# Operand loads split between cross attention's contexts, and the latent stage's transposes moved one slot behind their scores

## The reference, cut to what matters

```
x = layernorm(x + L0_xattn(x, ctx, ctx))       # 16 heads of 16, 361 context rows per batch
...
# L1_xattn: latents = x (100 rows per batch), ctx has 361 rows, 16 heads of 64
xn, ln = layer_norm(ctx), layer_norm(latents)
q = ln @ Wq;  k, v = split(concat(xn, ln) @ Wkv)          # 461 keys
sim = where(mask, (q * scale) @ k^T, -max)
out = layer_norm((softmax(sim) @ v) @ Wout)
x = layernorm(x + out)
```

## Time and profile before

| | |
|---|---|
| median of 3 runs | 2555.2 us |
| the profiled execution | 2563.16 us |
| its span in the trace | 2561.5 us |
| TensorE busy | 2135.1 us (83%) |
| VectorE, ScalarE, GpSimd busy | 1355.6, 1128.6, 474.4 us |
| granted clock, mean | 0.912 of full speed |
| cross attention, about | 590 to 1035 us |
| latent attention, about | 1359 to 2289 us |

### The profile page before, as it was taken

One profiled execution on the slowest core, in us unless ns is written; L12 is line 12 of the kernel. 1 busy time (PEld: TensorE's weight loads), 2 busy tenths in 40 slices (PEclk: granted clock), 3 DMA queues, 4 the chain that ended last, 5 costly groups with the idle time before them and its releaser, 6 DMA issues. The chain is left out here.

```text
span 2561.5 us, 48525 instructions
## 1 busy us (share of the span) xinstructions
PE 2135.1 (83%) x17362; PEld 1314.8 (51%) x17363; DVE 1355.6 (53%) x3264; ACT 1128.6 (44%) x2404; POOL 474.4 (19%) x533
## 2 busy tenths in 40 slices
PE   1888888864999999777777999999999999963992
PEld 0454555442666665554443555655555555552661
DVE  1577777751455555358883455555555555432223
ACT  0566666650555555135552444444444444420110
POOL 2455555510000000224440000000000000003002
PEclk9789999975999999779997999999999999966996
DMA  5000000006000000000000000000000000026101
GB/s 153 1 2 1 0 0 0 2 1 185 19 18 12 17 15 2 1 1 0 0 0 18 7 7 6 6 6 12 6 6 6 6 6 7 1 78 223 33 31 58
DMA packets 50461, 60.83 MB, mean 24 GB/s; under 512 B 9849, under 2 KB 44974, under 8 KB 49918
## 3 DMA queue, kind: packets, MB, share of 16 engines
q1 hardware_dynamic: 47366, 53.74, 6.8%
q0 software_dynamic: 3008, 5.91, 0.8%
HBM read 51.11 MB, written 8.52 MB: 23 GB/s over the span
## 5 line engine op out<-in xcount | busy, mean ns | idle before, releaser
L2155 DVE CUSTOM_DVE_ANT_0 la_pr<-la_pS,la_mb 100x461 f32<-100x461 f32 x256 | 148.1, 636 | 197.2 <-PE la_pS L2018 197.2
L2000 PE MATMUL la_side<-la_wkv,la_inT 128*128 128x512 f32 (+1 forms) x512 | 243.4, 598 | 0.0
L2256 ACT ACTIVATE la_pr<-la_pr,la_nm 100x461 f32<-100x461 f32 x256 | 171.9, 674 | 135.8 <-DVE la_nm L2155 135.8
L1988 PE MATMUL la_side<-la_inT,la_wkv 128*128 128x461 f32 x512 | 227.2, 566 | 0.8 <-ACT la_inT L2240 0.8
L2264 ACT COPY la_pT<-la_pPT 128x400 f32<-128x400 f32 x256 | 126.2, 493 | 165.4 <-PE la_pPT L2026 164.1
L2026 PEld LDWEIGHTS la_pPT<-io_ident,la_pr 100*128 100x128 f32 x1024 | 110.4, 144 | 149.0 <-issue 105.7
L1028 DVE TENSOR_REDUCE ca_nm<-ca_pS 100x2 f32<-100x722 f32 x128 | 116.2, 908 | 112.5 <-PE ca_pS L915 110.6
L2323 POOL TENSOR_TENSOR la_xb<-io_X,la_bo 100x256 f32<-100x256 f32 x16 | 11.6, 728 | 840.4 <-DVE io_X L2144 840.4
L2026 PE MATMUL la_pPT<-io_ident,la_pr 100*128 100x100 f32 x1024 | 137.5, 257 | 29.7 <-ACT la_pT L2264 18.4
L1100 ACT ACTIVATE ca_pr<-ca_pS,ca_nm 100x361 f32<-100x361 f32 x256 | 130.0, 561 | 64.4 <-DVE ca_nm L1028 62.6
L2117 DVE COPY la_v<-la_side 128x512 f32<-128x512 f32 (+1 forms) x128 | 87.8, 686 | 101.3 <-PE la_side L2000 101.2
(11 more groups left out here) (356 smaller groups left out, 4372.7 us busy)
## 6 DMA issues: line engine op xcount, KB each, us to landing
rf_w<-in_L_ffn_W SPq DMA_DIRECT2D x16, 1024.0 KB, 14.0
ca_cn<-in_ctx SPq DMA_DIRECT2D x16, 256.0 KB
la_cn<-in_ctx SPq DMA_DIRECT2D x16, 256.0 KB, 2.7
rows_in<-io_zero SPq DMA_DIRECT2D x20, 128.0 KB, 4.6
rb_xr<-rows_in POOLq DMA_DIRECT2D x20, 128.0 KB, 2.3
rows_out<-rb_yr SPq DMA_DIRECT2D x20, 128.0 KB, 1.7
ea_wcT<-in_t_L_ffn_conv_W SPq DMA_DIRECT2D x1, 2048.0 KB
la_wkv<-in_L_xattn_Wkv SPq DMA_DIRECT2D x1, 2048.0 KB
```

The lines of the kernel that those rows point to most:

```text
L1988: last = nc.tensor.matmul(pf[:, 0:SK], wkv[:, k, e * P:(e + 1) * P], inT[:, k, :], start=k == 0, stop=k == KD - 1)
L2000: last = nc.tensor.matmul(pf[0:keys[c], :], inT[:, k, c * P:c * P + keys[c]], wkv[:, k, o:o + 512], start=k == 0, stop=k == KD - 1)
L2155: ins = nc.vector.tensor_tensor_reduce(out=pr[m % 2][:, e, 0:SK], in0=pS[0:T, 2 * (m % 2) + e, 0:SK], in1=mb[b][:, :], scale=-1.0, scalar= ...
L2256: ins = nc.scalar.activation(pr[m % 2][:, e, 0:SK], pr[m % 2][:, e, 0:SK], ACT.Exp, scale=-1.0, bias=nm[m % 2][:, e:e + 1], accum_out=zs[m ...
```

## The change

1. **Loads in cross attention.** `Operands.load` is split into `one` per DMA. Cross attention's SP program goes over the 16 contexts, and puts up to three operand DMAs behind each context from that of batch 1 on (31 DMAs in all, so the last stand behind the context of batch 11).
2. **First latent context.** The tile `cn` of the latent stage, and the two DMAs that fill it for batch 0, become part of the latent operands; the stage's SP program starts with batch 1. VectorE waits for `32 * i` instead of `32 * i + 32`.
3. **Latent turns.** `pr` has four buffers. A slot turns the two pairs of the slot before it, and takes the values of the slot two before. The side steps have another order, each of the four turns now stands behind a step, and the order of VectorE's and ScalarE's programs follows. After batch 15 come one more slot of turns and two of values.

```
@@ cross_attention, sync
-                load(0)
-                for x in later:
-                    x.load(sp)
-                for i in range(1, 3):
+                todo = [(x, t, src) for x in later for t, src in x.pairs]
+                share = -(-len(todo) // (NB - 4))
+                for i in range(NB):
                     load(i)
-                with sp.Fori(3, NB) as i:
-                    load(i)
+                    if i:
+                        for x, t, src in todo[(i - 1) * share:i * share]:
+                            x.one(sp, t, src)
@@ latent_operands
+    w.cn = st.sb("cn", [P, 3, D])
+    w.pairs += [(w.cn[:, 0:2, :], d["ctx_1024"][0, 0:2 * P, :].rearrange("(c p) n -> p c n", p=P)),
+                (w.cn[0:SC - 2 * P, 2, :], d["ctx_1024"][0, 2 * P:SC, :])]
@@ latent_attention
+    ORDER = [["fk0", "fk1", "fk2", "fq0", "fk3"], ["by", "fv00", "fk4", "fv01", "fk5"],
+             ["fv10", "fk6", "fv11", "fk7", "fv20"], ["fq1", "fv21", "fv30", "fv31", "gl", "gc0", "gc1"]]
+        pr = [sb(f"pr{b}", [T, 2, KP_]) for b in range(4)]
@@ tensor
                     for j in range(MD):
-                        if j:
-                            both_values(i, b, j - 1)
+                        if j > 1:
+                            both_values(i, b, j - 2)
                         elif not first:
-                            both_values(i - 1, 1 - b, MD - 1)
+                            both_values(i - 1, 1 - b, j + 2)
...
-                            turn(i * MP + 2 * j + h // 2, h // 2, h % 2)
-                        for _, name, n in todo:
-                            step(name, n, i + turns.AHEAD[name[0]], turns.buffer(name, b))
+                        for h in range(4):
+                            some(h + 1)
+                            if j:
+                                turn(i * MP + 2 * j - 2 + h // 2, 2 * j - 2 + h // 2, h % 2)
+                            elif not first:
+                                turn(i * MP - 2 + h // 2, MP - 2 + h // 2, h % 2)
+                        some(9)
@@ vector
                         maxima(i, b, 2 * j + 1)
+                        some(2)
                         norm(i * MP + 2 * j, 2 * j)
-                        some(2)
+                        some(4)
                         norm(i * MP + 2 * j + 1, 2 * j + 1)
-                        some(3)
-                        if j == 1 and not first:
+                        if j == 2 and not first:
                             out_norm(i - 1)
-                        if j == 2 and not first:
+                        if j == 3 and not first:
                             x_norm(i - 1)
@@ scalar
                         for h in range(4):
-                            if h:
-                                some(2 + h)
-                            evac(i * MP + 2 * j + h // 2, h // 2, h % 2)
...
+                            some(h + 1)
+                            if j:
+                                evac(i * MP + 2 * j - 2 + h // 2, h // 2, h % 2)
...
+                            if h < 2:
+                                exps(i, 2 * j + h)
```

More of the change, by code:

```diff
@@ L81, in want, with one @@
         return t
+    def one(self, sp, t, src):
+        with self.st.nc.allow_non_contiguous_dma("small constants"):
+            dst = t[0:src.shape[0]] if len(t.shape) == len(src.shape) else t[:].rearrange("p a b -> p (a b)")
+            sp.dma_start(dst, src).then_inc(self.s_in, 16)
     def load(self, sp):
-        with self.st.nc.allow_non_contiguous_dma("small constants"):
-            for t, src in self.pairs:
-                dst = t[0:src.shape[0]] if len(t.shape) == len(src.shape) else t[:].rearrange("p a b -> p (a b)")
-                sp.dma_start(dst, src).then_inc(self.s_in, 16)
+        for t, src in self.pairs:
+            self.one(sp, t, src)
     def wait(self, eng):
@@ L1849, in __init__ @@
         self.g, self.f = [n for n in self.names if n[0] == "g"], [n for n in self.names if n[0] == "f"]
-        assert self.per % 2 == 0 and kinds[0] == "b" and kinds.count("b") == 1
+        assert self.per % 2 == 0 and kinds.count("b") == 1
         self.lead = 2 * len(self.g) + len(self.f) - 1
@@ L1860, in at @@
         if isinstance(i, int):
-            gone = len(self.g) if i == NB - 1 else 0
-            return self.At(self.lead + self.per * i + k - gone, None, self.per)
+            back = next(q for q, n in enumerate(self.names) if n[0] == "b")
+            if i == 0:
+                k += k < back
+            elif i == NB - 1:
+                k -= len(self.g) + back
+            return self.At(self.lead + self.per * i + k, None, self.per)
         return self.At(self.lead + k, i, self.per)
@@ L1909, in latent_attention @@
     keys = [min(P, SK - c * P) for c in range(NC)]
-    ORDER = [["by", "fk0", "fv00", "fk1", "fv01"], ["fk2", "fv10", "fk3", "fv11", "fq0"],
-             ["fk4", "fv20", "fk5", "fv21", "fq1"], ["fk6", "fv30", "fk7", "fv31", "gl", "gc0", "gc1"]]
+    ORDER = [["fk0", "fk1", "fk2", "fq0", "fk3"], ["by", "fv00", "fk4", "fv01", "fk5"],
+             ["fv10", "fk6", "fv11", "fk7", "fv20"], ["fq1", "fv21", "fv30", "fv31", "gl", "gc0", "gc1"]]
     MD = len(ORDER)
@@ L1925, in latent_attention @@
         zs = [sb(f"zs{b}", [T, 4]) for b in range(2)]
-        pr = [sb(f"pr{b}", [T, 2, KP_]) for b in range(2)]
+        pr = [sb(f"pr{b}", [T, 2, KP_]) for b in range(4)]
         pT = [sb(f"pT{b}", [P, 2, NC * T]) for b in range(2)]
@@ L1958, in load @@
                     sp.dma_start(cn[0:ckeys[2], 2, :], d["ctx_1024"][i, 2 * P:SC, :]).then_inc(s_cn, 16)
-                for i in range(3):
+                for i in range(1, 3):
                     load(i)
@@ L2011, in scores @@
                     if m == 0:
[L2012 removed]
+                        turns.wait_read(pe, s_R, i, "fv30")
                         turns.wait_read(pe, s_R, i, "fv31")
@@ L2054, in body, with some @@
                         todo = turns.steps(i, j)
-                        for h, upto in enumerate((2, 3, 4, 5)):
+                        def some(upto):
                             while todo and todo[0][0] < upto:
@@ L2066, in _ @@
                 over_batches(pe, body, 3)
+                both_values(NB - 1, 1, MD - 2)
+                for h in range(4):
+                    turn(NB * MP - 2 + h // 2, MP - 2 + h // 2, h % 2)
                 both_values(NB - 1, 1, MD - 1)
@@ L2075, in inputs @@
                 def inputs(i):
-                    dv.wait_ge(s_cn, 32 * i + 32)
+                    above(dv, s_cn, 32 * i)
                     dv.wait_ge(s_xs, i + 1)
@@ L2149, in maxima @@
                     dv.wait_ge(s_S, n + 1)
-                    above(dv, s_PTp, 2 * (n - 1))
+                    above(dv, s_PTp, 2 * (n - 3))
                     if m == 0:
@@ L2307, in _ @@
                         inputs(1)
-                ac.wait_ge(s_z, 4)
+                ac.wait_ge(s_z, 6)
                 over_batches(ac, body, 3)
+                sums(NB - 1, 1, MD - 2)
+                for h in range(4):
+                    evac(NB * MP - 2 + h // 2, h // 2, h % 2)
                 sums(NB - 1, 1, MD - 1)
@@ L2328, in _ @@
                     nc.gpsimd.memset(v[b][:, NC - 1, :], 0.0).then_inc(s_z, 1)
+                for b in range(4):
                     nc.gpsimd.memset(pr[b][:], 0.0).then_inc(s_z, 1)
                 stage(1)
+                stage(2)
                 residual(0)
-                stage(2)
-                residual(1)
-                with po.Fori(2, NB - 1) as i:
-                    stage(i + 1)
+                with po.Fori(1, NB - 2) as i:
+                    stage(i + 2)
                     residual(i)
+                residual(NB - 2)
                 residual(NB - 1)
```

28 lines of the change are left out of this document (13 added, 15 removed).

## The result

The changed kernel is slower: 2595.1 us (median of 4 runs, 2588.5 to 2603.8) beside 2557.8 us for the kernel before on the same chip (4 runs), a ratio of 1.0158, 95% interval 1.0136 to 1.0180. The forecast was 2566, in a range of 2539 to 2585: the sign was right, the size was not. The profiled execution took 2592.6 us, of which 2590.5 are the span, 29.0 more than before.

A forecast was written before the change was run, and what follows sets the result against it. It took TensorE's own work to bound the latent loop, with a 24.00 us context wait in cross attention. Gains of -47.0, +33.8 for batches 1 to 13 and +24.5 of clock gave +11.3: 2566 us, range 2539 to 2585.

The forecast's parts named there:

- Batch 15: Last latent batch: three waits go, a tail of turns and values is added; 45.5 us for 53.55, 8.0 less (3 to 11).
- The wait at the context: Cross attention, batch 0: TensorE's 24.0 us wait goes, and low clock behind it; together 31.3 us less.
- First latent context: Start of latent attention: VectorE's statistics begin 2.4 us earlier, inherited by later prologue steps; bounds 0 and 4.
- The gap at `gl`: Latent slot j = 3: TensorE stands 3.35 us for VectorE's chain; 4.1 us with gc1, in each of batches 0 to 13.
- The clock in the gap: Latent loop: the clock falls around gl's wait, 1.75 us lost per gap (bounds 0 and 3.4), 24.5 in 14 gaps.
- Rivals 1 and 2: Latent gap: 1, the clock holds, 2542 us, chance 0.15; 2, the clock costs only 0.85 per gap, 2554 us, chance 0.15.
- The bubbles: Latent loop: TensorE's small gaps before turns, waiting for norm or ScalarE's copy, go; 1.5 us less per batch, bounds 0 and 2.
- The `gc1` term: Latent slot j = 3: gc1 must wait until ScalarE has read gl's bank; 0.7 us more per batch.
- Batch 0 and batch 14: Latent batches: batch 0's first slot lacks turns and values, 3.3 us less; batch 14 has no gl, 2.0 less.
- Rival 4: Latent loop: ScalarE, with exponentials between its copies, holds up turns; 0.5 us in each of 60 slots, 2596 us, chance 0.10.

The follow-up runs named there:

- the third: The kernel before with only cross attention's operand DMAs shared out between the contexts, first latent context loaded as before: 2533.7 us, ratio 0.9907.
- the fourth: The kernel before with the latent layer's edits alone (late turns, new step order, four pr buffers), loads as before: 2621.8 us, ratio 1.0256.
- the eighth: The kernel before with one edit, VectorE copying fv31 ahead of apply_inputs in slot j = 3: 2597.7 us, ratio 1.0167.
- the seventh: The changed kernel with x_norm and apply_inputs early, two GpSimd memsets later, and ScalarE's copies ahead of exponentials in the last batch's slots 1 and 2: 2516.6 us.
- the sixth: The changed kernel with x_norm alone moved to the head of slot j = 3, apply_inputs staying at its end: 2582.8 us, ratio 1.0110.
- the fifth: The changed kernel with 36 unread transpositions put on TensorE ahead of gl's wait: 2573.3 us, ratio 1.0059.
- the first experiment: The changed kernel with VectorE's x_norm and apply_inputs moved to the start of slot j = 3, ahead of the maxima: 2521.8 us, ratio 0.9861.
- the second: The kernel before with both loading edits alone (operands in shares, first latent context with the operands), latent layer as before: 2534.9 us, ratio 0.9912.

## Why the prediction was wrong in size

The mechanism was right: `gl` waits for VectorE's chain behind the copy of `fv31`, in 14 batches, and the clock falls behind it. The costs of the wait were sized well: 5.1 us a batch was forecast (3.35 of path, 1.75 of clock), 5.4 measured. The step that failed is the sum of the gains. Batch 15 was put at -8.0 and brought nothing, the loads and the first context at -33.7 and brought -28.1, and the bubbles of the loop, net of `gc1`, at -0.8 a batch and brought -0.44. Term by term:

- **The wait at the context** (term -31.3): right that it goes and that nothing is late in its place; batch 0 of cross attention fell by 51.52 - 24.23 = 27.3, so 4.0 too much. Slots 1 to 3 take 11.4 us (4.12, 4.54, 2.72) where 8.3 stood, and slot 0 2.4. The forecast put the whole of the low clock down to the wait. It is low there without the wait: 0.50 from 590.00 to 606.06, and 0.71 in the first 12 us after the first scores, 606.06 to 618.00. How far it reaches differs by run: batch 0 took 24.2 to 24.7 us in eight kernels with the new loads and 27.4 in the third, and with the old loads 51.5, 52.0 and 47.5 (before, the fourth, the eighth).
- **First latent context** (-2.4): the wait went, and 1.67 us came back in the products, which now run beside the last of GpSimd's memsets. The forecast mentioned the two new memsets and priced them at nothing. Shown by the seventh.
- **The gap at `gl`** (3.35 of 4.1): the chain was right, step by step; 3.59 measured, since the products took 0.4 more beside `residual` (the sixth). Path cost 3.5 (the fifth).
- **The clock in the gap** (1.75): 1.85 measured (the fifth). Rivals 1 and 2 fall. Of the two readings behind the term, 1.7 us lost behind the idle time of self attention and up to 3.4 in batch 15, the first was the near one. In the example of the Trainium skill (TensorE: Matmul & The Clock Gate, section HAM oscillation) half of 1.67 us is lost in every pass. The trace agrees that the clock fell behind all 14 waits of 2.8 to 3.6 us; the size is twice that example's.
- **The bubbles** (-1.5 a batch, and +0.7 for `gc1`): -0.8 in sum was forecast, -0.44 measured (the first against before, 55.01 to 54.57). The `gc1` term is right (0.76 for 0.7): from `gl` to the values it takes 1.87 us in the first experiment (1905.52 to 1907.39) without a turn in between; before it took 1.87 with a turn, 1.1 without the turn and its wait. That leaves some 1.2 for the bubbles. The forecast's own items (0.14 three times, 0.4 twice, 0.1) add up to 1.3, which it rounded up to 1.5. The miss is 5 us in 13 batches.
- **Batch 0 and batch 14** (-3.3 and -2.0): slot 1 of batch 0 took 11.4 where 9.8 was set. Batch 14 starts in the slow stretch of the gap ahead, but that is 0.3 us of its 1.0: without the gap, in the first experiment, it takes 52.74 and not 52.1. They are 2.7 us together.
- **Batch 15** (-8.0): -0.1 up to `by`. This is the largest single miss beside the loop's. With no steps between them, turns behind ScalarE's exponentials stand 1.7 us apart, and the clock is 0.74. Slots 0 to 2 fell from 39.9 to 34.6, and the last slot and the tail took 18.9 where the last slot took 13.6 before. I had worked out 42.4 at full clock and 50 with much of it at half, and took 45.5 between; the stretch is worse than the second of these. Against the full-clock figures slots 0 and 2 took 10.1 and 9.8 for 8.2, slot 1 14.7 for 11.7, and the last slot with the tail 18.9 for 14.3; how much of that is the clock and how much the chain, no run parts. The batch differs by run: 53.6, 52.8, 51.2 and 51.2 us with the old turns (before, the second, third and eighth), 50.5 to 53.5 with the new ones and ScalarE's order unchanged. On average both are at 52.2 to 52.3, so the late turns brought nothing there.

Rival 4 gave 2596, as measured, but for a reason that isn't there: in the loop no turn's matmuls wait for ScalarE, and its weight loads do so 12 times, 2.4 us in all. A time alone would have named the wrong culprit; the wait's releaser tells them apart.

The misses are 5.6 (loads and context), 7.5 (loop), 2.7 (batches 0 and 14) and 7.3 (the end), 23 together, all to the same side. The loop's are some 0.15 for the gap, 0.10 for the clock and 0.36 for the bubbles, 0.6 in each of 13 batches. The rest of the 29 lies in the two medians of before, 2555.2 and 2557.8, and in how each profile stands to its median.

## What to carry to other kernels

When work is reordered on one engine, follow each wait of the busiest engine through the other engine's new program; a chain of small steps behind one copy was worth 5.4 us a batch, and moving two calls up made the same change 1.4% faster where it had been 1.6% slower. A repeated wait on TensorE costs its length and, mostly, some clock; if it can't be removed, even useless matmuls in it win part back. A sum of gains is only as good as the state that it assumes: two of the gains that fell short, at cross attention's start and in batch 15, lie in stretches where the granted clock was low (0.71 and 0.74) without the wait that the forecast removed. And the idle time of a window doesn't bound what small gaps are worth: from before to the first experiment, batches 1 to 12 lost 5.6 us at a clock of 1.00, of which 4.1 lay in TensorE's busy time (652.11 to 648.02) and 1.5 in its idle time.

## What the runs showed of the hardware

- A wait of 3.6 us a batch in a loop that is otherwise dense costs 1.85 us more by the clock, one of 1.9 us some 1.2 us in 12 of 14 batches and nothing in two. The slow stretch lies behind the wait: the granted clock is 1.00 from 1776.50 to 1780.16, while TensorE waits, and 0.61 in the 4.33 us from `gl` (1780.16 to 1784.49).
- VectorE's tensor_scalar from SBUF to SBUF is slowed beside GpSimd: 1.05 to 1.46 for three beside an addition (and the addition 0.72 to 1.04), 1.06 to 2.48 and 2.82 beside memsets. Its batch statistics beside GpSimd's memsets took 1.08 as ever. The Trainium skill (SBUF — State Buffer, section Who interferes with whom) says that the two share a port pair, which an instruction that uses it holds for its whole length, and that tensor_scalar can claim it; these numbers agree with it.
- Profiles of stages whose code is the same differ by 5 us and more: the first scores of cross attention came between 602.25 and 616.33 us. Landmarks inside the program resolve what four to six total times don't, but each is itself one run: batch 15 moves by 2 to 3 us with the granted clock.
